# Bigger filler products on TensorE in three context attentions and a causal one, and one score bank fewer

## The reference

```
layer 0, context:     q from x (512 rows), k, v from a context of 154 rows, a mask per key (all ones)
layer 1, causal:      q, k, v from x (512 x 512 scores, lower triangle)
layer 1, remembered:  q from x, k, v from the context; the keys are weighted and masked by a count
                      of how often each was chosen, added as a bias per key
layer 2, context:     q from x, k, v from the context, a mask per query and key (512 x 154)

scores = q @ k.T / sqrt(8) (+ mask); out = softmax(scores) @ v; x = layernorm(x + out @ w_o)
```

## Time and profile before

| | |
|---|---|
| median of 3 runs | 5115.67 us (5104.46 to 5119.01) |
| the profiled execution | 5115.46 us, of which the span of instructions is 5113.6 us |
| PE busy | 4108.0 us, 80% of the span |
| PE weight loads busy | 2386.7 us, 47% |
| DVE busy | 3161.2 us, 62% |
| ACT busy | 2577.4 us, 50% |
| POOL busy | 1272.7 us, 25% |

### The profile page before, as it was taken

How to read it: one execution, slowest core, us unless ns; L and a number is a source line. 1 busy time by engine, 2 the same in 40 slices (tenths; PEclk the granted TensorE clock), 3 DMA queues, 4 the chain that set the end, 5 groups by cost and what they waited for, 6 DMA issues and landing times. The chain is left out here.

```text
span 5113.6 us, 121487 instructions
## 1 busy us (share of the span) xinstructions
PE 4108.0 (80%) x46546; PEld 2386.7 (47%) x46580; DVE 3161.2 (62%) x5750; ACT 2577.4 (50%) x5318; POOL 1272.7 (25%) x2920
## 2 busy tenths in 40 slices
PE   2004867996767996786997669999999999999997
PEld 1003333333342322343443337777777777777775
DVE  8996335443427876435555327777777777777775
ACT  2034523442545876451224436666666666666665
POOL 0011101011212111210001134444444444444443
PEclk6556677555777988797997779999999999999998
DMA  1001123100213410303541000000000000000000
GB/s 45 0 0 33 35 64 78 39 14 17 51 34 75 89 27 14 68 10 78 141 136 34 5 23 29 6 10 24 6 28 6 10 24 6 10 25 6 29 6 11
DMA packets 139163, 171.79 MB, mean 34 GB/s; under 512 B 34631, under 2 KB 121779, under 8 KB 137436
## 3 DMA queue, kind: packets, MB, share of 16 engines
q1 hardware_dynamic: 138182, 164.06, 13.2%
q0 software_dynamic: 432, 0.23, 0.0%
HBM read 124.06 MB, written 32.89 MB: 31 GB/s over the span
## 5 line engine op out<-in xcount | busy, mean ns | idle before, releaser
L838 DVE TENSOR_REDUCE minus_max<-banks 128x1 f32<-128x512 f32 (+4 forms) x1152 | 622.4, 571 | 486.7 <-PE banks L667 475.2
L766 ACT ACTIVATE probs<-banks 128x512 f32<-128x512 f32 (+4 forms) x1152 | 615.9, 559 | 449.2 <-PE banks L635 440.3
L2972 POOL TENSOR_TENSOR loc_cos_part<-loc_cos_part,loc_sin_part 128x512 f32<-128x512 f32 x388 | 494.5, 1275 | 661.4 <-DVE loc_sin_part L3401 660.8
L635 PE MATMUL banks<-q_stack,k_stack 51*128 51x512 bf16 (+4 forms) x1152 | 448.7, 434 | 33.5 <-DMA q_stack<-max_rows 32.2
L667 PE MATMUL banks<-k_stack,q_stack 48*128 48x512 bf16 (+5 forms) x1536 | 445.6, 351 | 30.4 <-PEq L68 19.7
L703 PE MATMUL banks<-probs,pair_rows 128*32 128x256 f32 (+1 forms) x4352 | 406.1, 456 | 8.4 <-issue 8.4
L3045 PE MATMUL banks<-loc_w_qkv,loc_shifted 128*128 128x256 f32 x1552 | 388.3, 393 | 15.5 <-DMA loc_adder_of<-loc_head_ones 15.5
L3045 PEld LDWEIGHTS banks<-loc_w_qkv,loc_shifted 128*128 128x128 f32 x1552 | 281.7, 191 | 54.0 <-issue 16.1
L3434 DVE TENSOR_TENSOR loc_headsT<-banks,loc_sum_inv 128x512 f32<-128x512 f32 x192 | 132.6, 691 | 280.4 <-ACT loc_sum_inv L3306 280.4
L3426 DVE TENSOR_REDUCE loc_minus_max<-banks 128x4 f32<-128x384 f32 x386 | 197.0, 552 | 150.8 <-PE banks L3112 150.0
L2012 PE MATMUL banks<-identity,srt_b 128*128 128x128 f32 x64 | 11.3, 322 | 344.5 <-DVE srt_b L2283 344.5
(11 more groups left out here) (507 smaller groups left out, 9250.7 us busy)
## 6 DMA issues: line engine op xcount, KB each, us to landing
expert_share<-limited_rows SPq DMA_DIRECT2D x136, 256.0 KB, 4.0
expert_w<-in_L_ffn_pairs_dram SPq DMA_DIRECT2D x84, 192.0 KB, 2.4
q_stack<-q_pieces SPq DMA_DIRECT2D x38, 384.0 KB, 6.3
loc_w_qkv<-in_L_ffn_Wqkv_dram SPq DMA_DIRECT2D x7, 1536.0 KB, 7.5
expert_share<-grouped_rows SPq DMA_DIRECT2D x32, 256.0 KB, 4.3
k_stack<-k_pieces SPq DMA_DIRECT2D x20, 384.0 KB, 9.6
q_pieces<-q_parts SPq DMA_DIRECT2D x19, 384.0 KB, 2.6
q_stack<-max_rows SPq DMA_DIRECT2D x384, 3.0 KB
```

The lines of the kernel that those rows point to most:

```text
L635: nc.tensor.matmul(t_bank(n, k, e)[:, q0:S], k_stack[rows_e, k0:k0 + P], q_stack[rows_e, q0:S], start=plain, stop=True, skip_group_check=T ...
L766: nc.scalar.activation(probs_of(n, k, e)[0:kn, q0:S], t_bank(n, k, e)[0:kn, q0:S], ACT.Exp, scale=scale).then_inc(s["exp_done"], 1)
L838: nc.vector.tensor_reduce(minus_max[:, n % 2, 1 - i, qs[0]:qs[0] + len(qs)], view, AX.X, ALU.max, negate=True).then_inc(s["max_done"], 1)
L2972: nc.gpsimd.tensor_tensor(cos_part[:, tiles, :], cos_part[:, tiles, :], sin_part[:, tiles, :], ALU.add).then_inc(s["summed"], 1)
```

## The change

The filler multiplies the first 128 columns of the first batch's first q piece (the stationary side) with all 512 of its columns, so both sides are data, and has 512 columns instead of 256. In the context attentions it also stands in each half step of the loop over slots, right behind `direct`: 3 x 128 = 384 products more, 456 in all. It writes to bank 4 there; so the direct scores have two banks instead of three, and `direct` of half step u waits for the maximum of half step u-2. The causal attention keeps three banks, its filler stays in the prologue and writes to bank 7.

```diff
         x_bank, o_bank = g.bank[2], g.bank[7]
-        t_banks, d_banks = (g.bank[5], g.bank[6], g.bank[0]), (g.bank[1], g.bank[3], g.bank[4])
+        t_banks = (g.bank[5], g.bank[6], g.bank[0])
+        d_banks = (g.bank[1], g.bank[3]) if context else (g.bank[1], g.bank[3], g.bank[4])
+        awake_bank = g.bank[4] if context else o_bank
...
         def d_bank(n, k, i):
-            return d_banks[unit(n, k, i) % 3]
+            return d_banks[unit(n, k, i) % len(d_banks)]
...
                 def direct_masks(n, k, i):
-                    after(pe, "max_done", unit(n, k, i) - 2)
+                    after(pe, "max_done", unit(n, k, i) + 1 - len(d_banks))
...
                     if plain:
-                        after(pe, "max_done", unit(n, k, i) - 2)
+                        after(pe, "max_done", unit(n, k, i) + 1 - len(d_banks))
...
                 def keep_awake():
 
-                    nc.tensor.matmul(o_bank[:, 0:S // 2], g.ident_bf[:, :], stacks.parts[which][0][:, 0, 0:S // 2],
-                                     start=True, stop=True, skip_group_check=True)
+                    some = stacks.parts[which][0][:, 0, :]
+                    nc.tensor.matmul(awake_bank[:, :], some[:, 0:P], some[:, 0:S], start=True, stop=True,
+                                     skip_group_check=True)
...
                             turned(n, k, i)
                             if ahead < N:
                                 direct(ahead, k, i)
+                            if context:
+                                keep_awake()
                             at = place(n, k, i)
```

## The result

The change takes 5176.41 us (median of 4 runs, 5170.63 to 5181.57), the kernel before 5113.19 us in the same comparison (4 runs, 5104.46 to 5119.01): a ratio of 1.0124, 95% interval 1.0099 to 1.0148. It is slower, by 63 us; 65.8 us were forecast. The profiled executions differ by 55.2 us (spans 5113.6 and 5168.8 us).

The account below looks back on a forecast made before the run. PE was taken to set the pace, at half clock in places. Layer 0 +1.7, remembered +21.8, layer 2 +37.2 and causal +5.1 us summed to +65.8 on 5115.46, so 5181 us; range 5085 to 5210.

Parts of the forecast that it names:

- Sign and sum: Whole kernel: slower by 65.8 us, to 5181 us; chance of slower by more than 0.3% was 0.74.
- No rival happened: Causal attention wakes up: 5084 us, chance 0.15; fillers fit gaps everywhere: 5103, 0.08; clock does not rise: 5275, 0.06.
- The reading of the clock: Unmasked loops before: clock rose at dense values' products, fell in thin half steps (means 0.67, 0.89); fillers lift it to full.
- The price of a filler at full clock: Context loops: 0.31 us before values or rows, 0.22 before a mask product, 0.48 at place 0 of unmasked quads.
- The masked loop: Layer 2 context attention, middle twelve quads: 1.99 us more per quad, +23.9 us, with no clock to gain.
- The first two quads: Start of each context loop: +5.1 us in layer 0 and remembered, +5.4 us in layer 2.
- The waits for sent maxima: Unmasked attentions: each wait gives back 1.7 us, leaving 7.3 us, added to both layer 0 and remembered.
- The middle of layer 0: Layer 0 context attention, middle twelve quads: 123.07 us becomes 110.2 + 7.3 at full clock, so -5.6 us.
- The remembered middle: Remembered attention, middle twelve quads: 105.79 us becomes 117.5, so +11.7 us.
- Two banks: Direct scores in context attentions: no cost in the loop, about 0.6 us in layer 0's prologue.
- The causal rival: Causal loop: 24 dense prologue products wake it to full clock, 97 us saved, kernel 5084 us; chance 0.15.
- One argument against it: Against the causal loop waking: its first quad lacks values, and the clock falls in such stretches, as at each attention's end.

Follow-up runs that it names:

- e4: The change with loop fillers in the two unmasked context attentions only, the masked one keeping its prologue fillers: 5144.57 us, 1.0054 against the kernel before.
- e1: The change with the stationary operand of every filler put back to the identity; size, place and number kept: 5176.68 us, 1.0109 against the kernel before.
- e5: The change with loop fillers only at places 4, 5 and 6 of a quad in the unmasked context attentions: 5105.02 us, 0.9967 against the kernel before.
- e9: Against the change: no fillers in context loops; causal fillers in each half step of the first two quads only, two banks there: 5102.13 us, 0.9955 against before.
- e10: Against the change: no context loop fillers; causal ones in the first two quads, then every fourth half step, two banks there: 5068.43 us, 0.9886 against before.

## Why the prediction was right

**Sign and sum.** +65.8 us were forecast and +63 measured (medians), +55 in the profiled pair. No rival happened: the causal loop stayed at 0.50, the clock did rise, and the fillers had a price. The reading of the clock, for which the earlier trace rows give only means, is borne out by the trace of the kernel before: in a layer 0 quad it rose at 529.0 us, among the values' products, and fell at 532.4, in PE's wait ahead of the heads, with none of those since 529.9. That the sum came so close is in part luck: the first two quads missed by +4.2 us in layer 0 and by -5.5 in layer 2, and one profile of the kernel before, with one unmasked middle 12 us above the mean of eight profiles and the other 8 below it, was the base of it all.

**The price of a filler at full clock** was taken from rows in which no filler stood, and held: 0.32 us ahead of values and rows (0.31 forecast), 0.23 ahead of a mask product (0.22). A masked quad takes 12.90 us (12.83), an unmasked one 9.43 (9.18). Of the 0.25 us between, half is idle time ahead of the heads, 0.88 us where the forecast left 0.75, and half is the eight fillers themselves, 2.94 us of PE's time where 2.82 were forecast. By the Trainium skill's rule (TensorE: Matmul & The Clock Gate, on the back-to-back issue gap) each would have cost 0.22 us; the trace agrees where the next product is of the filler's own shape, as ahead of masks (0.23 us), and on the mean in the causal loop (0.22 to 0.24), and not where the tile changes (0.32).

**The masked loop**, +24.6 us (23.9 forecast), is the surest part: its clock was at 1.00, and e4, which leaves these fillers out, is 32 us faster than the change; 25.6 of them are its loop of sixteen quads (199.16 us in the windows above, 173.59 in e4).

**The first two quads** were mis-sized both ways. I priced unmasked ones at half clock for eight fillers and full clock for the rest (+5.1); they took +9.3 and +6.0, because the clock stayed at 0.50 in all of layer 0's 26.07 us (26.07 and 26.06 in e1 and e4, so this is no draw). In layer 2 I forecast +5.4 and measured -0.1: the clock rose in the first quad (0.94 over both). That is a draw: with the same number and places of fillers e1 took 26.53 us there at 0.82, +2.6. What makes the clock come early there in some executions is open. Why the same prologue with loop fillers leaves layer 0 at 0.50 for two quads, when without them it takes 15.70 us, is not settled.

**The waits for sent maxima** were mis-sized: 7.3 us in each unmasked attention, measured some 0.2 us in layer 0 and 3.9 in the remembered one. The slower slots gave more slack than the 1.7 us per wait that I took, and not all of the 6.1 and 4.6 us that I had read off was a wait: PE stood 4.49 and 3.24 us there, and the rest went with the clock, which was 0.50 in the 6.43 us behind the longer wait. e5 confirms the place, since the waits return at 7.64 us a quad. Slower quads (9.43 for 9.18, 3.0 us in twelve) make up for part of it, and in layer 0 a first middle quad still partly at half clock (1.8 us).

**The middle of layer 0** was right in number (-5.6, measured -7.9) and wrong in meaning. I called the clock's gain real there, reading 123.07 us as this loop's time. Eight profiles say 102.4 to 123.1 for the same products. The remembered middle (+11.7, measured +11.2) is the mirror image: the 105.79 us that I started from were that loop's best draw. The fillers trade a clock that comes and goes for a steady one at 115 to 117 us, and that is dearer than the mean without.

**Two banks** cost nothing in the loop and 0.7 to 1.0 us in each context prologue (0.6 forecast, in layer 0 alone); in the loops DVE was never what PE waited for.

**The causal rival** had the mechanism and the wrong trigger. Full clock is worth even more than the 31% I took, and the loop can hold it (12.64 us a quad, -37%). Twenty-four prologue fillers do not start it, though; fillers in the loop do, after two quads. One argument against it was misread: the clock does not fall at the end of each attention, it stayed at 1.00 in the last two quads of layer 2.

## What to carry to other kernels

Work whose only use is to raise TensorE's clock pays only where the clock is low, and costs its full length wherever TensorE is the bound: put it in stages that the profile shows at half clock, in places where the engine waits anyway, and thin it until the clock just holds with some reserve. Before crediting a change with a gain in such a stage, profile the kernel without it more than once: the clock's course differs between executions of the same instructions, and a good draw in the base hides a gain as a poor one feigns it. A loop can have two lasting paces, and one wait may tip it from the fast to the slow one.

## What the runs showed of the hardware

- A loop in which PE was busy for 311.28 of 312.78 us had a granted clock of 0.50 throughout; the same loop with no product added ran three quads at 1.00 once fillers had preceded it, and fell for good in the quad with a 0.88 us wait for a transfer, 2.7 us after the wait (e9, one execution).
- With a filler every fourth half step it went through waits of 0.63 and 0.88 us at 1.00 (e10).
- An unmasked context loop without fillers ran for many quads on end at either of two paces, 10.24 us at 0.67 or 7.47 to 8.8 us at 0.84 to 1.00.
- The identity as stationary operand served as well as data (e1: 5176.68 against 5176.41 us).
- The kernel before, 25 runs of it on one chip, spread from 5091.00 to 5141.56 us, 1%. With fillers in all the context loops, the change's four lie within 11 us and e1's four within 20, which is too few runs to call it steadier. The middles of the unmasked loops without fillers, 102 to 123 us, and the first two quads of the masked one, 18.4 to 25.3 us, are parts of such a spread that the profiles show.
